# A graph-attention layer with residual norm on one core: two row buffers, copies put between signs, and positive sums that start on the first mask

## The chip, the cores and the metric

The kernel runs on one core of a Trainium2 chip. The metric is device time in microseconds (us), the median of several executions. The profile and the trace are those of one execution.

## The reference

One graph-attention layer over N = 8192 nodes with 256 features, H = 4 heads of 64 features, then a residual and a layer norm:

```python
xt  = einsum('ni,hio->hno', x, W)                    # 4 heads, 64 features each
src = einsum('hnf,hf->hn', xt, a[:, :64])
dst = einsum('hnf,hf->hn', xt, a[:, 64:])
e   = leaky_relu(src[:, :, None] + dst[:, None, :], 0.2)
e   = where(adj > 0, e, -inf)                        # adj is 8192 x 8192, int32
out = layernorm(x + concat_heads(softmax(e, axis=2) @ xt))
```

`exp(leaky_relu(s + d))` is a product of a factor of the row and a factor of the column, with one pair of factors where `s + d` is positive and another where it is not. So the kernel needs no exponential per edge: it splits the edges of a head by the sign of `s + d`, and sums the rows of two prepared tables (values and, as a 65th column, the denominators) over the positive and over the other edges.

## The kernel before

**Preparation.** About the first 216 us transform x, make the factors and write four tables of parts (V, 16 bit, a high and a low part of each number, for positive and for negative) to DRAM. The first adjacency blocks are converted, transposed and packed in AT.

**Main part.** The output rows are cut into NC = 8 chunks of 1024 rows. A chunk is done in H = 4 passes, one per head h, 32 passes in all. A pass has NG = 16 steps g, and a step handles 512 columns of the adjacency (B = 4 blocks of 128) for the chunk's 1024 rows. In each step:

- ScalarE (ACT, L392, `signs`) makes the sign of `s + d` for 4 blocks in an even step and for 3 in an odd one, in a ring `sgn` of NB = 4 steps. It may start step n when TensorE has ended the sums of step n-4 (`sums_done`).
- VectorE (DVE) makes the fourth block of an odd step (L552, `compares`), then the mask of the positive edges (L560, `masks_of`, `pos_done`), and last the mask of the others (L567, `rest_of`, `neg_done`). Between the two masks stand, in an even step, the comparison for the next step and one conversion of the next chunk's adjacency (L480, L482, `convert`), and in an odd step one `keep` (L496), which packs transposed blocks in AT.
- TensorE (PE), in an even step, first transposes the converted blocks (L719, `turn_masks`, waits for the conversion), and then multiplies: 64 matmuls of 128x128 masks by 128x130 of V (L754, `sums`): for each of 4 blocks and 8 row tiles t, one for the positive and one for the negative mask. They wait for `neg_done` of their step, which comes last.

**Between two passes.** The sums of pass p-1 lie in PSUM (`acc`) and have to be read before pass p may overwrite them. ScalarE copies the low parts to `u` in three portions (L405, `low`), after its step-1 signs of the new pass. Each portion waits for TensorE: the first two for `part_done` after 3/8 and 6/8 of the old step 15, the third for its end. VectorE adds the high parts (L574, `high`): portion 0 after its first mask of step 1, portions 1 and 2 after its second one. TensorE's step 0 waits for them one by one (`u_done`, before row tiles 0, 3 and 6). Then VectorE weighs, joins, inverts, divides and adds the residual (L582, L589, L593, L599, L608), one each in steps 2 to 6.

**Between two chunks.** One buffer `y` holds the chunk's x rows (loaded by a DMA of GpSimd's queue, L321, `load_res`), to which the four heads are added. In pass h = 0 of the next chunk VectorE takes the moments (L613, steps 8 and 9, and L619, step 10), GpSimd makes the scale and the shift (L327 to L333, `deviation`), ScalarE normalises 8 tiles, two after each of the steps 12 to 15 (L411, `normalise`, waits for `shift_done`), and GpSimd stores y (L337), waits for the store's landing and loads the next rows into the same buffer.

SyncE's queue loads V tables (one for each step), sign rows and adjacency blocks. The order on each engine is written out by hand. In the first chunk 10 or 11 blocks are converted and kept per pass in place of 8, and in the last one none.

Of the kernel before, what the change touches and what calls it, by code (L numbers as in the profile page):

```python
# [5 lines left out]
def gat_residual_norm(nc: bass.Bass, x: bass.AP, adj: bass.AP, W: bass.AP, a: bass.AP, out: bass.AP):  # L6
    fp32 = mybir.dt.float32
# [8 lines left out]
    ACT = mybir.ActivationFunctionType  # L16
# [30 lines left out]
    with ctx:  # L47
        def sb(name, shape, dt):
            return ctx.enter_context(nc.sbuf_tensor(name, shape, dt))

        def sem(name):
            return ctx.enter_context(nc.semaphore(name))
# [14 lines left out]
        shift = sb("shift", [P, T], fp32)  # L67
        big = sb("big", [P, 24144], fp32)

        def words(start, n):  # L70
            return big[:, start:start + n]
# [3 lines left out]
        sgn = words(8320, 4096).bitcast(i8).rearrange("p (n b i) -> p n b i", n=NB, b=B)  # L75
        y = words(12416, 2048).rearrange("p (t f) -> p t f", t=T)
        u = words(14464, 1040).rearrange("p (q v) -> p q v", v=VO)
# [67 lines left out]
        added = sem("added")  # L145
        res_in = sem("res_in")
        stats_done = sem("stats_done")
# [64 lines left out]
        def scalar_blocks(g):  # L212
            return B - g % 2
# [87 lines left out]
        def _(pool):  # L301
# [17 lines left out]

            def load_res(c):  # L320
                pool.dma_start(y[:, :, :], res_v[c]).then_inc(res_in, 16)  # L321

# [11 lines left out]

            def store(c):
                pool.wait_ge(norm_done, T * c + T)
                pool.dma_start(out_v[c], y[:, :, :]).then_inc(out_done, 16)  # L337
# [11 lines left out]
            with pool.Fori(1, NC) as c:  # L349
                chunk(c)  # L350
            deviation(NC - 1)
            store(NC - 1)
            pool.wait_ge(out_done, 16 * NC)


        @block.scalar
        def _(act):
# [29 lines left out]

            def signs(n, g, h):
                act.wait_ge(sums_done, n + 1)
                for b in range(scalar_blocks(g)):  # L390
                    r = (g * B + b) * H + h
                    ins = nc.scalar.activation(sgn[:, g % NB, b, :], srow[:, h % 2, :], ACT.Sign,  # L392
                                               bias=dflat[:, r:r + 1], scale=-1.0)
                ins.then_inc(sgn_done, 1)

# [11 lines left out]

            def normalise(c, ts):
                act.wait_ge(shift_done, 2 * c + 2)
                for t in ts:  # L410
                    nc.scalar.activation(y[:, t, :], y[:, t, :], ACT.Identity, bias=shift[:, t:t + 1],  # L411
                                         scale=rstd[:, t:t + 1]).then_inc(norm_done, 1)

            def chunk(c, first=False):
# [12 lines left out]
            act.wait_ge(lo_done, NG + 2)  # L427
            act.wait_ge(U2_done, 2 * NG)
            chunk(0, first=True)
            with act.Fori(1, NC) as c:  # L430
                chunk(c)
            for part in range(3):
                low(NP - 1, part)
            normalise(NC - 1, range(T))


        @block.vector
        def _(dve):
# [162 lines left out]

            def add_on(p, ec, eh):

                dve.wait_ge(res_in, 16 * ec + 16)
                dve.wait_ge(tr_done, p + 1)
                u4 = u.rearrange("p (t c) v -> p t c v", c=2)
                yh = y[:, :, eh * O:(eh + 1) * O]
                nc.vector.tensor_tensor(out=yh, in0=yh, in1=u4[:, :, 1, 0:O], op=ALU.add).then_inc(added, 1)  # L608

            def moments(c, ts):  # L610
                dve.wait_ge(added, 4 * c + 5)
                for t in ts:
                    nc.vector.bn_stats(stats[:, t, :], y[:, t, :]).then_inc(stats_done, 1)  # L613

# [7 lines left out]
            def chunk(c, plane, first=False, after_first=False, more=True):  # L622

                last = [UN * c + 2 * g + 4 for g in range(NG)]
                for h in range(H):
                    dve.wait_ge(row_in[h % 2], 32 * c + 16 * (h // 2 + 1))
                    for g in range(NG):
# [24 lines left out]
                        if ended:  # L652
                            if g == 1:
                                high(p, 1)
                                high(p, 2)
                            if g == 2:
                                weigh(p, ec, eh)
                            if g == 3:
                                join(p)
                            if g == 4:  # L660
                                inverse(p)
                            if g == 5:
                                divide(p)
                            if g == 6:
                                add_on(p, ec, eh)
                        if h == 0 and not first:
                            if g == 8:
                                moments(c - 1, range(0, 4))
                            if g == 9:
                                moments(c - 1, range(4, T))  # L670
                            if g == 10:
                                spread(c - 1)
# [13 lines left out]
            divide(NP - 1)  # L686
            add_on(NP - 1, NC - 1, H - 1)
            moments(NC - 1, range(T))
            spread(NC - 1)


        @block.tensor
        def _(pe):
# [118 lines left out]
```

## Time and profile before

| | |
|---|---|
| median of 3 runs | 2369.2 us (2365.97 to 2369.42) |
| profiled execution | 2367.08 us, span 2364.6 us |
| PE, DVE, ACT busy | 2108.9, 2098.4, 2012.6 us |
| matmuls L754, signs L392 | 32768, 1792 |
| TensorE's granted clock, mean | 0.962 |
| DMA, mean | 199 GB/s |

Rows of the windows view give busy times of each engine in a stretch. Rows of the timeline give start, duration, engine, line, operation, operands and count, and in brackets how long the engine had idled and who released it. A VectorE or ScalarE operation's duration overlaps the next one's start by about 0.1 us, so the distance of two starts is the better price.

### The profile page before, as it was taken

Reading aid. Unit: us, or ns where it says so; the run is one execution under the profiler, and the core shown is the slowest. Engines: PE = TensorE matmul, PEld = TensorE weight load, DVE = VectorE, ACT = ScalarE, POOL = GpSimd, SP = SyncE. Lnnn points to the kernel's source line nnn. Section 1 sums busy time; section 2 is a strip of 40 time slices with the busy share of each in tenths; the row PEclk is TensorE's granted clock in tenths of the full one; section 3 lists DMA queues with packets and bytes.
Section 4 is the critical chain, followed back from the end, with each engine's and each line's share of the span. In section 5 each row is a group of like instructions: output and inputs, shape, how many; then the busy total and the mean of one; then the engine's idle time right before and its main releaser. Section 6 shows DMA issues by size and latency. Waiting matters only on the chain.

```text
span 2364.6 us, 79642 instructions
## 1 busy us (share of the span) xinstructions
PE 2108.9 (89%) x34180; PEld 2063.9 (87%) x34180; DVE 2098.4 (89%) x2334; ACT 2012.6 (85%) x2045; POOL 120.0 (5%) x88
## 2 busy tenths in 40 slices
PE   7602999998999899998999999998999899998996
PEld 6502999998999899998999999998999899998996
DVE  4597999998999899998999899998999899987785
ACT  2235798898999899998999899998999899999995
POOL 0062000001000100001000100001000100001000
PEclk9855999999999999999999999999999999999998
DMA  8647776766666576666666576666666576533210
GB/s 296 221 180 284 275 247 231 241 218 213 209 200 221 176 239 208 209 202 212 211 199 209 188 236 205 213 203 209 210 203 221 176 236 206 194 84 105 84 52 19
DMA packets 236588, 469.77 MB, mean 199 GB/s; under 512 B 14656, under 2 KB 23104, under 8 KB 236224
## 3 DMA queue, kind: packets, MB, share of 16 engines
q1 hardware_dynamic: 231600, 447.53, 57.3%
q0 software_dynamic: 4352, 16.78, 2.0%
q8 instruction: 286, 4.69, 0.8%
q14 instruction: 78, 0.64, 0.1%
q10 hardware_dynamic: 272, 0.13, 0.0%
HBM read 438.83 MB, written 25.56 MB: 196 GB/s over the span
## 4 chain that ended last, share of the span: by engine, by line
PE 48%; ACT 16%; DVE 14%; issue 8%; POOL 2%; DVEq 0%; POOLq 0%; ACTq 0%
PE acc L754 46%; ACT big L392 15%; DVE big L560 4%; DVE big L567 4%; PE tp L719 2%; DVE nat L482 1%; ACT big L411 1%; DVE stats L613 1%; POOL shift L330 1%; DVE big L552 1%; DVE big L582 1%; DVE nat L480 1%; POOL rstd L329 0%; DVE AT L496 0%; DVE big L589 0%
## 5 line engine op out<-in xcount | busy, mean ns | idle before, releaser
L754 PE MATMUL acc<-big 128*128 128x130 f16 x32768 | 1933.5, 221 | 84.1 <-DVE big L567 53.7
L754 PEld LDWEIGHTS acc<-big 128*128 128x128 fp8e5 x32768 | 1901.0, 98 | 107.2 <-issue 103.6
L392 ACT ACTIVATE big<-big,d_all 128x1024 int8<-128x1024 f32 x1792 | 1881.4, 1139 | 60.9 <-PE acc L754 58.4
L560 DVE SCALAR_TENSOR_TENSOR big<-big,AT 128x1024 uint32<-128x1024 uint32 x512 | 627.4, 1225 | 168.6 <-ACT big L392 157.7
L567 DVE SCALAR_TENSOR_TENSOR big<-AT,big 128x1024 uint32<-128x1024 uint32 x512 | 627.0, 1225 | 4.5
L719 PE MATMUL tp<-ident,nat 128*128 128x128 f32 x1024 | 158.8, 278 | 133.0 <-DVE nat L480 115.9
L719 PEld LDWEIGHTS tp<-ident,nat 128*128 128x128 f32 x1024 | 109.7, 142 | 142.9 <-issue 132.5
L552 DVE TENSOR_SCALAR big<-big,d_all 128x1024 uint8<-128x1024 f32 x256 | 193.2, 755 | 0.0
L480 DVE TENSOR_SCALAR nat<-raw 128x2048 fp8e4<-128x2048 int32 x128 | 177.0, 1386 | 6.9 <-DMA raw<-in_adj_dram 6.5
L482 DVE TENSOR_SCALAR nat<-raw 128x2048 uint8<-128x2048 int32 x128 | 177.8, 1389 | 0.0
L496 DVE SCALAR_TENSOR_TENSOR AT<-AT,tp 128x512 uint32<-128x512 uint32 x224 | 154.8, 691 | 1.5
L405 ACT ACTIVATE big<-acc 128x390 f32<-128x390 f32 (+2 forms) x128 | 44.1, 382 | 76.0 <-PE acc L754 76.0
L327 POOL TENSOR_SCALAR rstd<-mv 128x8 f32<-128x8 f32 x8 | 7.3, 911 | 1925.0 <-DVE mv L619 1925.0
L411 ACT ACTIVATE big<-big,shift,rstd 128x256 f32<-128x256 f32 x64 | 34.3, 587 | 67.6 <-POOL shift L333 67.6
L385 ACT ACTIVATE big<-AT 128x1040 f16<-128x1040 f32 x16 | 17.4, 1088 | 62.4 <-POOL AT L318 42.3
L710 PE MATMUL acc<-big,AT 128*128 128x264 f32 x256 | 62.9, 401 | 4.2 <-DVE d_all L469 4.2
L710 PEld LDWEIGHTS acc<-big,AT 128*128 128x128 f32 x256 | 48.8, 196 | 15.5 <-issue 5.1
L467 DVE COPY big<-acc 128x1024 f32<-128x1024 f32 x16 | 19.6, 1225 | 39.4 <-PE acc L710 39.4
L574 DVE TENSOR_TENSOR big<-big,acc 128x390 f32<-128x390 f32 (+2 forms) x128 | 48.7, 424 | 6.0 <-ACT big L405 6.0
L363 ACT ACT_TABLE_LOAD x8 | 10.3, 1283 | 42.1 <-PE acc L702 42.1
L316 POOL TENSOR_TENSOR AT<-big 128x1024 f32 x16 | 38.7, 2421 | 40.2 <-DVE big L530 28.9
L582 DVE TENSOR_TENSOR big<-big,ab 128x1040 f32<-128x1040 f32 x32 | 39.7, 1241 | 0.0
(48 smaller groups left out, 364.2 us busy)
## 6 DMA issues: line engine op xcount, KB each, us to landing
raw<-in_adj_dram SPq DMA_DIRECT2D x256, 1024.0 KB, 5.4
big<-v_parts SPq DMA_DIRECT2D x512, 260.0 KB, 3.8
v_parts<-big SPq DMA_DIRECT2D x16, 1040.0 KB, 4.2
big<-s_rows SPq DMA_DIRECT2D x32, 512.0 KB, 5.8
AT<-in_x_dram SPq DMA_DIRECT2D x16, 512.0 KB, 4.0
big<-in_x_dram POOLq DMA_DIRECT2D x8, 1024.0 KB, 7.6
out_dram<-big POOLq DMA_DIRECT2D x8, 1024.0 KB, 7.9
big<-in_L_gnn_W_dram SPq DMA_DIRECT2D x2, 128.0 KB, 2.6
```

Of the source, the lines that this page charges most:

```text
L392: ins = nc.scalar.activation(sgn[:, g % NB, b, :], srow[:, h % 2, :], ACT.Sign, bias=dflat[:, r:r + 1], scale=-1.0)
L411: nc.scalar.activation(y[:, t, :], y[:, t, :], ACT.Identity, bias=shift[:, t:t + 1], scale=rstd[:, t:t + 1]).then_inc(norm_done, 1)
L480: nc.vector.tensor_scalar(to.bitcast(fp8e4), of, 0.0, 1.0, ALU.is_gt, ALU.add, saturate=False).then_inc(conv_done, 1)
L482: nc.vector.tensor_scalar(to, of, 0.0, 59.0, ALU.is_gt, ALU.add).then_inc(conv_done, 1)
L496: nc.vector.scalar_tensor_tensor(out=to, in0=to, scalar=EDGE[1 - plane], in1=of, op0=ALU.bitwise_and, op1=ALU.bitwise_or).then_inc(at_done, 1)
L552: ins = nc.vector.tensor_scalar(sgnu[:, g % NB, b, :], srow[:, h % 2, :], dflat[:, r:r + 1], 255.0, ALU.is_gt, ALU.mult)
L560: nc.vector.scalar_tensor_tensor(out=word(sgn, g % NB), in0=word(sgn, g % NB), scalar=EDGE[plane], in1=edges(g), op0=ALU.bitwise_and, op1= ...
L567: nc.vector.scalar_tensor_tensor(out=word(neg, g % NB), in0=edges(g), scalar=EDGE[plane], in1=word(sgn, g % NB), op0=ALU.bitwise_and, op1= ...
L582: nc.vector.tensor_tensor(out=u4, in0=u4, in1=w.unsqueeze(3).broadcast_to([P, T, 2, VO]), op=ALU.mult).then_inc(wu_done, 1)
L710: ins = nc.tensor.matmul(acc[:, 2 + b, 0:WX], xT[n][:, k, b, :], Wx[:, k, :], start=(k == 0), stop=(k == KF - 1))
L719: ins = nc.tensor.transpose(tp[:, u % 2, b * P:(b + 1) * P], natw[u % 2][:, b * P:(b + 1) * P], ident[:, :])
L754: return nc.tensor.matmul(acc[:, k, o:o + 2 * VO], m[:, g % NB, b, t * P:(t + 1) * P], Vr[:, v:v + 2 * VO], start=opens, stop=False, skip_ ...
```

## The change

Four edits:

1. **Two row buffers.** `y` becomes a pair, the second one in 2048 more words of `big`. `load_res(0)` and `load_res(1)` are both issued at the start, and after the store of chunk c the rows of chunk c+2 are loaded. `res_in` becomes two semaphores.
2. **Normalising later.** ScalarE normalises chunk c-1 in pass h = 1 of chunk c, one tile after each of the steps 8 to 15, where it was two tiles after each of the steps 12 to 15 of pass h = 0.
3. **Low copies between signs.** The three portions of `low` stand after the first, second and third sign of step 2, where they stood together ahead of step 2.
4. **Positive sums first.** In steps 1 to 14 TensorE does the 32 matmuls of the positive mask first and waits for `pos_done` alone, then waits for `neg_done` and does the 32 negative ones. Steps 0 and 15 keep their order and wait for both.

ScalarE's loop body has two chunks now (3 turns where there were 7), and so has GpSimd's.

```diff
-        y = words(12416, 2048).rearrange("p (t f) -> p t f", t=T)
+        y = [words(start, 2048).rearrange("p (t f) -> p t f", t=T) for start in (12416, 24144)]
...
             pool.wait_ge(U2_done, 2 * NG)
-            load_res(0)
+            load_res(0, 0)
+            load_res(1, 1)
 
-            def chunk(c):
-                deviation(c - 1)
-                store(c - 1)
-                pool.wait_ge(out_done, 16 * c)
-                load_res(c)
+            def chunk(c, n):
+                deviation(c)
+                store(c, n)
+
+                pool.wait_ge(out_done, 16 * c + 16)
+                load_res(c + 2, n)
...
-                        signs(p * NG + g, g, h)
-                        if g == 1 and not (first and h == 0):
-                            for part in range(3):
-                                low(p - 1, part)
-                        if g in (12, 13, 14, 15) and h == 0 and not first:
-                            normalise(c - 1, (2 * g - 24, 2 * g - 23))
+                        act.wait_ge(sums_done, p * NG + g + 1)
+                        for b in range(scalar_blocks(g)):
+                            ins = sign(g, h, b)
+                            if b == scalar_blocks(g) - 1:
+                                ins.then_inc(sgn_done, 1)
+                            if g == 2 and b < 3 and not (first and h == 0):
+                                low(p - 1, b)
+                        if h == 1 and g >= 8 and not first:
+                            normalise(c - 1, 1 - n, (g - 8,))
...
             def sums(p, g):
-                pe.wait_ge(neg_done, p * NG + g + 5)
+                pe.wait_ge(pos_done, p * NG + g + 1)
                 pe.wait_ge(v_in[g], 16 * p + 16)
...
                 else:
-                    for b in range(B):
-                        for cd in range(2):
+                    for cd in range(2):
+                        if cd:
+                            pe.wait_ge(neg_done, p * NG + g + 5)
+                            pe.sem_inc(pe_passed, 1)
+                        for b in range(B):
                             for t in range(T):
                                 ins = add(b, cd, t)
```

ScalarE at the start of a pass in the first chunk, before (L392 signs, L405 low copies; the second row of each pair is the rest of a step's signs):

```order
L392 ACTIVATE big<-big,d_all 128x1024 [waits sums_done,row_in0]
L392 ACTIVATE big<-big,d_all 128x1024 x3
L392 ACTIVATE big<-big,d_all 128x1024 [waits sums_done]
L392 ACTIVATE big<-big,d_all 128x1024 x2
L405 ACTIVATE big<-acc 128x390 [waits added,part_done]
L405 ACTIVATE big<-acc 128x390 [waits part_done]
L405 ACTIVATE big<-acc 128x195 [waits sums_done]
L405 ACTIVATE big<-acc 128x65
L392 ACTIVATE big<-big,d_all 128x1024 [waits sums_done]
L392 ACTIVATE big<-big,d_all 128x1024 x3
```

The same place in the changed kernel:

```order
L394 ACTIVATE big<-big,d_all 128x1024 [waits sums_done,row_in0]
L394 ACTIVATE big<-big,d_all 128x1024 x3
L394 ACTIVATE big<-big,d_all 128x1024 [waits sums_done]
L394 ACTIVATE big<-big,d_all 128x1024 x2
L394 ACTIVATE big<-big,d_all 128x1024 [waits sums_done]
L406 ACTIVATE big<-acc 128x390 [waits added,part_done]
L394 ACTIVATE big<-big,d_all 128x1024
L406 ACTIVATE big<-acc 128x390 [waits part_done]
L394 ACTIVATE big<-big,d_all 128x1024
L406 ACTIVATE big<-acc 128x195 [waits sums_done]
L406 ACTIVATE big<-acc 128x65
L394 ACTIVATE big<-big,d_all 128x1024
```

Three of the four signs of step 2 now stand ahead of the last low copy, and the fourth behind it.

TensorE in steps 0 to 2 of the second pass, before (L719 transposes, L754 sums):

```order
L754 MATMUL acc<-big 128x130 [waits neg_done,v_in0,u_done]
L754 MATMUL acc<-big 128x130 x23
L754 MATMUL acc<-big 128x130 [waits u_done]
L754 MATMUL acc<-big 128x130 x23
L754 MATMUL acc<-big 128x130 [waits u_done]
L754 MATMUL acc<-big 128x130 x15
L754 MATMUL acc<-big 128x130 [waits neg_done,v_in1]
L754 MATMUL acc<-big 128x130 x63
L719 MATMUL tp<-ident,nat 128x128 [waits at_done,conv_done]
L719 MATMUL tp<-ident,nat 128x128 x3
L754 MATMUL acc<-big 128x130 [waits neg_done,v_in2]
L754 MATMUL acc<-big 128x130 x63
```

The changed kernel in steps 0 to 2 of the second pass, from the last part of step 0 on:

```order
L760 MATMUL acc<-big 128x130 [waits u_done]
L760 MATMUL acc<-big 128x130 x15
L725 MATMUL tp<-ident,nat 128x128 [waits at_done,conv_done]
L725 MATMUL tp<-ident,nat 128x128 x3
L760 MATMUL acc<-big 128x130 [waits pos_done,v_in1]
L760 MATMUL acc<-big 128x130 x31
L760 MATMUL acc<-big 128x130 [waits neg_done]
L760 MATMUL acc<-big 128x130 x31
L760 MATMUL acc<-big 128x130 [waits pos_done,v_in2]
L760 MATMUL acc<-big 128x130 x31
L760 MATMUL acc<-big 128x130 [waits neg_done]
L760 MATMUL acc<-big 128x130 x31
```

A step's 64 matmuls are now two runs of 32 with a wait each, and where a step has transposes, they still stand ahead of both with their wait for the conversion.

## Rows read from the trace of the kernel before

**Rows 1.** Windows: window, length, busy us of PE, PEld, DVE, ACT, POOL, clock, DMA.
```profile
297.70:365.00 67.30, 64.43 (x1070) 63.00 (x1067) 65.19 (x71) 61.16 (x63) 0.00 (x0) 1.00 0.74 241
...
499.50:2095.10 1595.60, 1519.63 (x25340) 1495.51 (x25340) 1485.54 (x1656) 1462.13 (x1486) 50.99 (x36) 0.99 0.63 206
...
902.40:966.50 64.10, 62.79 (x1059) 61.85 (x1057) 60.70 (x66) 60.05 (x62) 0.00 (x0) 1.00 0.64 209
...
1030.60:1105.90 75.30, 66.41 (x1059) 64.47 (x1058) 63.52 (x81) 65.53 (x72) 8.17 (x6) 0.95 0.57 189
1105.90:1168.60 62.70, 62.06 (x1056) 61.83 (x1057) 62.29 (x67) 58.11 (x58) 0.65 (x1) 1.00 0.70 233
2095.10:2342.20 247.10, 236.34 (x4098) 235.08 (x4096) 190.04 (x209) 234.76 (x241) 7.37 (x6) 0.99 0.25 70
```
**Rows 2.** Waits of chunks 1 to 6 (499.5 to 2095.1): us in total, times, longest.
```profile
DVE big L560 <- ACT big L392: 104.1, 41, 4.8
...
ACT big L411 <- POOL shift L333: 53.6, 6, 9.4
ACT big L405 <- PE acc L754: 53.4, 53, 1.7
...
PE acc L754 <- DVE big L567: 45.5, 68, 3.8
...
PE acc L754 <- DVE big L574: 19.0, 14, 2.1
```
**Rows 3.** Timeline, one undisturbed pair of steps.
```profile
1003.46 7.39 ACT L392 ACTIVATE big<-big,d_all 128x1024 int8<-128x1024 f32 x7 [0.33 <-PE acc L754]
...
1006.40 1.24 DVE L560 SCALAR_TENSOR_TENSOR big<-big,AT 128x1024 uint32<-128x1024 uint32 x1
...
1007.34 7.44 PE L754 MATMUL acc<-big 128*128 128x130 f16 x128
...
1013.46 1.23 DVE L560 SCALAR_TENSOR_TENSOR big<-big,AT 128x1024 uint32<-128x1024 uint32 x1
```
**Rows 4.** Timeline, from pass h = 3 to pass h = 0 of the next chunk.
```profile
1028.01 0.50 ACT L405 ACTIVATE big<-acc 128x390 f32<-128x390 f32 x1 [1.51 <-PE acc L754]
...
1030.59 7.54 PE L754 MATMUL acc<-big 128*128 128x130 f16 x128
1030.68 36.50 ACT L392 ACTIVATE big<-big,d_all 128x1024 int8<-128x1024 f32 x35
1031.24 0.96 DVE L574 TENSOR_TENSOR big<-big,acc 128x390 f32<-128x390 f32 x3
1034.97 1.23 DVE L560 SCALAR_TENSOR_TENSOR big<-big,AT 128x1024 uint32<-128x1024 uint32 x1 [2.77 <-ACT big L392]
```
**Rows 5.** Timeline, the rest of that pass h = 0 and the start of h = 1.
```profile
1072.11 0.65 PE L719 MATMUL tp<-ident,nat 128*128 128x128 f32 x4 [0.52 <-DVE nat L480]
...
1073.30 7.43 PE L754 MATMUL acc<-big 128*128 128x130 f16 x128 [0.54 <-DVE big L567]
...
1081.22 1.09 ACT L411 ACTIVATE big<-big,shift,rstd 128x256 f32<-128x256 f32 x2 [9.44 <-POOL shift L333]
...
1088.64 6.41 PE L754 MATMUL acc<-big 128*128 128x130 f16 x64 [3.82 <-DVE big L567]
...
1102.84 1.18 ACT L405 ACTIVATE big<-acc 128x390 f32<-128x390 f32 x4
...
1108.10 6.13 PE L754 MATMUL acc<-big 128*128 128x130 f16 x104 [0.64 <-DVE big L574]
```
**Rows 6.** Last chunk: a wait of the timeline, and its sum over 2095.1 to 2342.2.
```profile
2139.43 1.09 ACT L411 ACTIVATE big<-big,shift,rstd 128x256 f32<-128x256 f32 x2 [3.25 <-POOL shift L333]
...
ACT big L405 <- PE acc L754: 9.2, 6, 6.3
```
**Rows 7.** The page: a group of part 5 and a DMA issue of part 6.
```profile
L363 ACT ACT_TABLE_LOAD x8 | 10.3, 1283 | 42.1 <-PE acc L702 42.1
...
big<-in_x_dram POOLq DMA_DIRECT2D x8, 1024.0 KB, 7.6
```

More of the change, by code:

```diff
@@ L67, in gat_residual_norm @@
         shift = sb("shift", [P, T], fp32)
-        big = sb("big", [P, 24144], fp32)
+        big = sb("big", [P, 26192], fp32)
         def words(start, n):
@@ L145, in gat_residual_norm @@
         added = sem("added")
-        res_in = sem("res_in")
+        res_in = [sem("res_in0"), sem("res_in1")]
         stats_done = sem("stats_done")
@@ L318, in _, with load_res @@
                     nc.gpsimd.tensor_copy(U2[n][:, :, :, O], e_row(e2, g)).then_inc(U2_done, 1)
-            def load_res(c):
-                pool.dma_start(y[:, :, :], res_v[c]).then_inc(res_in, 16)
+            def load_res(c, n):
+                pool.dma_start(y[n], res_v[c]).then_inc(res_in[n], 16)
             def deviation(c):
@@ L333, in deviation, with store @@
                 nc.gpsimd.tensor_tensor(out=shift[:, :], in0=shift[:, :], in1=rstd[:, :], op=ALU.mult).then_inc(shift_done, 1)
-            def store(c):
+            def store(c, n):
                 pool.wait_ge(norm_done, T * c + T)
-                pool.dma_start(out_v[c], y[:, :, :]).then_inc(out_done, 16)
+                pool.dma_start(out_v[c], y[n]).then_inc(out_done, 16)
             pool.wait_ge(lo_done, NG + 2)
             pool.wait_ge(U2_done, 2 * NG)
-            load_res(0)
-            def chunk(c):
-                deviation(c - 1)
-                store(c - 1)
-                pool.wait_ge(out_done, 16 * c)
-                load_res(c)
[L349 to L352, printed above, removed]
+            load_res(0, 0)
[5 more added lines that the diff above has]
+                load_res(c + 2, n)
+            with pool.Fori(0, NC // 2 - 1) as i:
+                chunk(2 * i, 0)
+                chunk(2 * i + 1, 1)
+            for c in (NC - 2, NC - 1):
+                deviation(c)
+                store(c, c % 2)
             pool.wait_ge(out_done, 16 * NC)
@@ L386, in _, with sign @@
                     nc.scalar.activation(V_part(n, 2), rows_of(U2[n]), ACT.Copy, scale=1.0 / LOW).then_inc(hi_done, 1)
[L388 to L394, printed above, removed]
+            def sign(g, h, b):
+                r = (g * B + b) * H + h
+                return nc.scalar.activation(sgn[:, g % NB, b, :], srow[:, h % 2, :], ACT.Sign,
+                                            bias=dflat[:, r:r + 1], scale=-1.0)
             def low(p, part):
@@ L406, in low, with normalise, chunk @@
                 ins.then_inc(low_done, 1)
-            def normalise(c, ts):
+            def normalise(c, n, ts):
                 act.wait_ge(shift_done, 2 * c + 2)
                 for t in ts:
-                    nc.scalar.activation(y[:, t, :], y[:, t, :], ACT.Identity, bias=shift[:, t:t + 1],
+                    nc.scalar.activation(y[n][:, t, :], y[n][:, t, :], ACT.Identity, bias=shift[:, t:t + 1],
                                          scale=rstd[:, t:t + 1]).then_inc(norm_done, 1)
-            def chunk(c, first=False):
+            def chunk(c, n, first=False):
                 for h in range(H):
@@ L428, in _ @@
             act.wait_ge(U2_done, 2 * NG)
-            chunk(0, first=True)
-            with act.Fori(1, NC) as c:
-                chunk(c)
+            chunk(0, 0, first=True)
+            with act.Fori(0, NC // 2 - 1) as i:
+                chunk(2 * i + 1, 1)
+                chunk(2 * i + 2, 0)
+            chunk(NC - 1, 1)
             for part in range(3):
                 low(NP - 1, part)
-            normalise(NC - 1, range(T))
+            normalise(NC - 1, (NC - 1) % 2, range(T))
         @block.vector
@@ L600, in divide, with add_on, moments @@
                                         in1=rden[:, :].unsqueeze(2).broadcast_to([P, T, O]), op=ALU.mult).then_inc(tr_done, 1)
-            def add_on(p, ec, eh):
-                dve.wait_ge(res_in, 16 * ec + 16)
+            def add_on(p, ec, eh, n):
+                dve.wait_ge(res_in[n], 8 * (ec - n) + 16)
                 dve.wait_ge(tr_done, p + 1)
                 u4 = u.rearrange("p (t c) v -> p t c v", c=2)
-                yh = y[:, :, eh * O:(eh + 1) * O]
+                yh = y[n][:, :, eh * O:(eh + 1) * O]
                 nc.vector.tensor_tensor(out=yh, in0=yh, in1=u4[:, :, 1, 0:O], op=ALU.add).then_inc(added, 1)
-            def moments(c, ts):
+            def moments(c, n, ts):
                 dve.wait_ge(added, 4 * c + 5)
                 for t in ts:
-                    nc.vector.bn_stats(stats[:, t, :], y[:, t, :]).then_inc(stats_done, 1)
+                    nc.vector.bn_stats(stats[:, t, :], y[n][:, t, :]).then_inc(stats_done, 1)
             def spread(c):
@@ L664, in chunk @@
                             if g == 6:
-                                add_on(p, ec, eh)
+                                add_on(p, ec, eh, 1 - plane if h == 0 else plane)
                         if h == 0 and not first:
                             if g == 8:
-                                moments(c - 1, range(0, 4))
+                                moments(c - 1, 1 - plane, range(0, 4))
                             if g == 9:
-                                moments(c - 1, range(4, T))
+                                moments(c - 1, 1 - plane, range(4, T))
                             if g == 10:
@@ L686, in _ @@
             divide(NP - 1)
-            add_on(NP - 1, NC - 1, H - 1)
-            moments(NC - 1, range(T))
+            add_on(NP - 1, NC - 1, H - 1, 1)
+            moments(NC - 1, 1, range(T))
             spread(NC - 1)
```

2 lines of the change are left out of this document (added).

## Prediction
> **What bounds the kernel now.** I read the windows view first, cut where a pass of TensorE starts. The six chunks 1 to 6 take 1595.6 us, 265.9 each, and they are two thirds of the time [rows 1]. Inside a chunk the four passes differ, and that is the point to see: h = 0 takes 75.3 us, h = 1 takes 62.7, and h = 2 (and h = 3, with the same length) 64.1 [rows 1].
>
> Next I asked what each engine would need alone. **TensorE:** the h = 1 pass holds a single wait inside, 0.64 us [rows 5], so a pass without waits is 62.70 - 0.64 = 62.06 us, a chunk 248.2. **VectorE:** a pair of steps, from the first mask of an even step to the next one with no idle time, is 1013.46 - 1006.40 = 7.06 us [rows 3], 56.5 for 8 pairs. The six pieces of work on the old pass add some 4.5 (VectorE is busy 60.7 in h = 2 [rows 1]), the moments about 3.2 more in h = 0: about 247 per chunk. **ScalarE:** 35 signs run in 36.50 [rows 4], 1.043 each, so 56 are 58.4. Four low copies in a row take 1.18 and two normalised tiles 1.09 [rows 5], so a chunk is 4 x 59.6 + 8 x 0.54 = 242.7. So all three have nearly the same load, TensorE's being the largest, and the 17.7 us above it in each chunk (265.9 - 248.2) are waits that go round between the engines.
>
> The waits view says which [rows 2]: ScalarE waits 53.6 us for the shift, in 6 waits of some 9, and 53.4 for TensorE ahead of the low copies. VectorE waits 104.1 for signs. TensorE waits 45.5 and 19.0 for VectorE. The timeline shows the two places. At a pass boundary ScalarE is done with step 1, waits 1.51 for the first portion and more for the others, and starts the signs of step 2 only at 1030.68. VectorE, which has ended its high parts by then, idles 2.77 until 1034.97 [rows 4]. It then has 7.06 us of work per pair against TensorE's 7.76 (62.06/8) plus the work on the old pass, so it can't make it up, and TensorE loses 2.0 per pass (64.1 - 62.06). In h = 0 ScalarE stands 9.44 us in front of its first normalised tile, VectorE starves, TensorE idles 3.82, and its next 64 matmuls take 6.41 us where 128 usually take 7.44 [rows 3, 5].
>
> **The change part by part.** *Normalising in h = 1* (edit 2; edit 1 makes it possible, since the buffer is needed for the next chunk otherwise). The shift is ready two thirds through h = 0, so the wait of about 9 goes whole. The 4.4 us of normalising stay on ScalarE, one pass later. In h = 0 the excess over the bare pass is 75.3 - 62.06 = 13.2. One part remains: VectorE's moments make it late for step 10, where TensorE waits 0.52 + 0.54 [rows 5]. I keep 1.1.
>
> *Low copies between signs* (edit 3). ScalarE's three waits at the boundary are now filled by signs it would have had to do anyway. It may start step 2 when the old step 14 ends, a step (half of 7.44) and four transposes (0.5) before step 0 of the new pass, at 1026.4. Four signs and the copies then end by 1032.5 against 1034.9, so VectorE's wait of 2.77 shrinks to some 0.3. That is the shape the h = 1 pass has today (four copies without waits at 1102.84, and no stall behind the one of 0.64) [rows 5]. So in h = 2 and h = 3 the 2.0 us go.
>
> *What comes instead.* In h = 1 ScalarE gets 4.3 us more, and regains 0.46 per pair (7.76 - 7.30 for 7 signs), 1.8 over these four. It arrives at h = 2 late by 2.5. VectorE then is late with the high parts, which TensorE's step 0 waits for. It ends portion 1 at 1031.24 + 0.47 = 1031.7, and row tile 3 is due 24 matmuls after 1030.59, at 1032.0 [rows 4], a slack of 0.3; in steps 0 and 1 about 0.5 is regained. So TensorE loses 2.5 - 0.3 - 0.5 = 1.7 there. The moments also leave VectorE late at the boundary to h = 1. After step 10 three pairs regain 2.1 of some 3.2, and I take 0.8 for what is left over the slack. A chunk becomes 248.2 + 1.1 + 0.8 + 1.7 = 251.8, a gain of 14.1, times six 84.6.
>
> *Positive sums first* (edit 4). It lets a step start on the first mask, and the second one may come 32 matmuls later (1.9 us). In an even step, though, the sums stand behind transposes that wait for the conversion, which comes just ahead of the second mask, so there the gain is under 1 us of slack. In odd steps the conversion is not in the way. By the steps above most of the 45.5 us that TensorE waits for the second mask [rows 2] are gone already, so I count this edit nothing by itself (bounds 0 and -1 per pass). Of its cost: the same matmul count; a slot of PSUM is revisited after 8 matmuls where it was 16, while steps 0 and 1 together (step 0 revisits after 2) take 7.54 against 7.44 for an ordinary pair [rows 3, 4], so 0 to 0.1 per step. 8 is nearer to 16 in effect, since the inner loop is unchanged, and I take 0; the other end, 0.1 x 14 x 32 = 45 us, is a rival. The extra wait in the middle I price at 0: step 0 has two such waits and is at most that 0.1 longer.
>
> *Last chunk.* No conversions, so ScalarE sets the pace (busy 234.8 of 247.1 [rows 1]). Its waits go: 3.25 for the shift, 9.2 - 7.2 = 2.0 at the three inner boundaries (the rest of the 9.2 is the end of the program) [rows 6], and 2.8 at the first boundary, as in rows 4. Gain 8. *First chunk.* VectorE is the bound (65.2 of 67.3 [rows 1]), and only its idle time for signs at the boundaries goes: 3 in three passes. *Second load at the start:* 1 MB, 7.6 us to landing [rows 7], while adjacency and V loads are waited for; between 0 and 7.6, I take 1. The end of the program is as before.
>
> Sum against the profiled execution: 2367.1 - 84.6 - 8 - 3 + 1 = 2272.5. The median lies 2.1 above that execution, so I give **2274**.
>
> **The clock.** In h = 0, which holds the shift wait, the mean clock is 0.95, in h = 1 and h = 2 it is 1.00 [rows 1]. After 3.82 us idle 64 matmuls took 6.41 [rows 5], 100 ns each against 58 (7.44 for 128 [rows 3]), so most of them ran at the 1.2 GHz level; the waits for high parts, up to 2.1 [rows 2], lie at the start of h = 1 and leave it at 1.00. The waits that I leave are at most 1.7, so no drop is in the sum. The Trainium skill ("TensorE: Matmul & The Clock Gate", Part 1) says that idleness takes TensorE to half clock and that activity gives it back. By that rule the trace agrees, and should a remaining wait cost a drop per chunk, 2.7 us each by rows 5, the sum would be 16 higher.
>
> **The rivals.**
> - *Everything is hidden.* VectorE's slack may be larger than I read, since edit 4 loosens it. Then a chunk is 248.2: 106 for six, 9 and 5 elsewhere, **2250**. For it: the h = 1 pass of today. Against: the moments' stall at step 10 waits for a conversion, which edit 4 does not touch.
> - *ScalarE's backlog stays.* Its reserve is 5.5 us per chunk; if copies between signs cost more than in a row, the 2.5 us of h = 1 are not regained and each of three further boundaries costs 1.5. Chunk 256.3: 58 for six, **2306**.
> - *Slower matmuls* by the revisit after 8, as priced above, up to 45: **2319** at most, 2296 halfway.
> - *The shift wait is only moved* (the second buffer does not free ScalarE, since a store or load is late): the chunk keeps its 265.9 and only the low copies gain, which VectorE loses again: no change. Against it: the normalising now stands 20 steps behind the moments.
> - *Slower: function tables.* ScalarE alternates between Sign and Copy or Identity. Per chunk there are 4 x 6 + 16 = 40 such switches where there were 16. Would each load a table for 1.283 us [rows 7], ScalarE's chunk would be 242.7 + 51 = 294, 28 over today's chunk: **2560**. The point where it turns slower is 18 loads per chunk. Against it: the 8 loads of this trace all have line L363, in the preparation, although 16 switches per chunk are there already. The Trainium skill ("ScalarE activation tables: per-element evaluation and per-set limits", "What a function is on this engine") says that functions of different sets are one load of 1283 ns apart and that those of one set need no switch. By that rule the three functions share a set, the trace agrees, and it adds nothing.
>
> **How the numbers follow.** Forecast, 2260 to 2290: 0.62. Everything hidden: 0.14. Backlog: 0.15. Slower matmuls: 0.05. Only moved: 0.02. Function tables: 0.02. Change and no change can be told apart at 0.2%, 4.7 us; all cases but the last two lie below 2364, so faster 0.96, same 0.02, slower 0.02. The range reaches from the first rival (2250) to just short of the backlog's 2306: 2250 to 2302, with the forecast, the hidden case and a part of the backlog's in it.
>
> **What would show it.** Right: the h = 0 pass near 63.2, h = 1 near 62.9, h = 2 near 63.8, h = 3 near 62.1; no ScalarE wait for the shift except the last; its wait ahead of the low copies near nothing; VectorE's wait for signs under 30 us in chunks 1 to 6; clock 1.00 throughout; still 8 table loads. Wrong: passes of 64 or more in h = 2 and 3 (backlog), more than 7.5 us per 128 matmuls (revisit), or a wait of TensorE in the middle of steps.

## The result, and the profile after

The changed kernel takes 2387.3 us (median of 4 runs, 2381.95 to 2399.94) against 2368.7 for the kernel before: a ratio of 1.0088, 95% interval 1.0047 to 1.013. It is slower by about 0.9%, where 4% faster was forecast. The profiled execution is the longest of the four, 2399.9 us with a span of 2398.1. Its spread of 18 us is new as well; the kernel before had 3.5.

The windows view of the changed kernel, cut at the starts of TensorE's passes as in [rows 1] (columns as there): first the second pass of chunk 0, then chunks 1 to 6 together, one pass each of h = 2, h = 0 and h = 1, and the last chunk.

```profile
298.40:363.60 65.20, 63.50 (x1071) 63.03 (x1069) 65.20 (x71) 61.51 (x64) 0.00 (x0) 1.00 0.75 249
495.90:2134.20 1638.30, 1530.12 (x25343) 1519.41 (x25342) 1492.70 (x1656) 1466.62 (x1489) 58.63 (x36) 0.97 0.62 201
907.70:976.30 68.60, 63.73 (x1058) 63.27 (x1058) 63.56 (x68) 61.67 (x62) 0.00 (x0) 0.97 0.65 205
1044.60:1112.60 68.00, 63.58 (x1058) 63.12 (x1059) 63.86 (x81) 60.30 (x60) 8.10 (x4) 0.98 0.62 197
1112.60:1180.90 68.30, 63.71 (x1058) 63.26 (x1058) 60.15 (x65) 62.30 (x67) 1.86 (x2) 0.97 0.67 213
2134.20:2376.20 242.00, 235.30 (x4096) 234.53 (x4094) 190.37 (x209) 231.51 (x239) 6.48 (x5) 0.99 0.24 67
```

The pattern of before (75.3, 62.7, 64.1) is gone. Every pass of chunks 1 to 6 now takes about 68 us, whatever its h. The first and the last chunk are shorter than before. So the loss has nothing to do with heads, moments or normalising: it is the same 5 to 6 us in each of the 24 passes of the middle, on top of the 62 to 63 a pass should take.

The waits of chunks 1 to 6, to be laid beside [rows 2]:

```profile
ACT big L394 <- PE acc L760: 167.1, 159, 7.7
DVE big L566 <- ACT big L394: 142.6, 103, 6.2
PEld tp L725 <- issue: 107.0, 23, 5.9
PE tp L725 <- issue: 91.6, 21, 4.7
```

ScalarE's waits for the shift (53.6) and ahead of the low copies (53.4) have vanished, and so have TensorE's for VectorE (45.5 and 19.0). In their place TensorE idles 91.6 us in 21 waits that end with an "issue": nothing in the profile was missing, its own queue had not yet handed out the next instruction. ScalarE and VectorE then wait for TensorE. The timeline of the boundary that ends pass h = 3:

```profile
1034.81 4.35 PE L760 MATMUL acc<-big 128*128 128x130 f16 x72
...
1036.87 0.50 ACT L406 ACTIVATE big<-acc 128x390 f32<-128x390 f32 x1 [0.25 <-PE acc L760]
...
1041.22 1.23 DVE L566 SCALAR_TENSOR_TENSOR big<-big,AT 128x1024 uint32<-128x1024 uint32 x1 [0.55 <-ACT big L394]
...
1043.73 0.74 PE L725 MATMUL tp<-ident,nat 128*128 128x128 f32 x4 [4.57 <-issue]
...
1044.54 8.91 PE L760 MATMUL acc<-big 128*128 128x130 f16 x128
...
1049.86 7.39 ACT L394 ACTIVATE big<-big,d_all 128x1024 int8<-128x1024 f32 x7 [5.56 <-PE acc L760]
```

The steps of the prediction are all there: the low copies no longer wait (0.25 for 1.51), and VectorE's idle time before step 2 is 0.55 for 2.77 [rows 4]. But TensorE stands still for 4.57 us between the last sum of the old pass and the first transpose of the new one. Its next 128 matmuls take 8.91 us for 7.54, and the granted clock of these passes is 0.97 to 0.98, where it was 1.00 in h = 1 and h = 2 before.

At that point of the code there is only one thing: the back edge of TensorE's loop over the passes (L794, L783 in the kernel before). The query for one line shows its instructions on TensorE's queue (count, then duration in ns as min/median/max). The kernel before:

```profile
L783 PEldq COMPARE_BRANCH  x24: 88/358/1329, 569.3 to 2094.1; - x24
```

The changed kernel:

```profile
L794 PEldq COMPARE_BRANCH  x24: 88/5140/6483, 557.2 to 2132.8; - x24
```

The branch takes 5.14 us where it took 0.36. The 24th is the exit. And TensorE's queue for instructions has moved more, though the same matmuls are issued; the page of the kernel before and of the changed one:

```profile
q8 instruction: 286, 4.69, 0.8%
```

```profile
q8 instruction: 309, 5.06, 0.8%
```

That is 23 packets of 16 KB more, as many as the main loop has taken back edges. Of the four edits only edit 4 touches TensorE's program. It gives each of the 16 steps a second wait with its semaphore instruction (steps 0 and 15 have both ahead of their sums), and the body needs 4 register operations more: it grows from 2169 to 2189 records of TensorE and its queue. The transposes are not moved. The order rows ahead of the prediction could suggest it, since they show transposes ahead of step 2 for the kernel before and ahead of step 1 for the changed one; but in the second pass both kernels have them ahead of step 1 (at 302.17 and 302.86 us).

### The profile page after: what moved, and what is told of

It reads as the page before. It is cut to its first block, busy times and chain, and to the rows that moved or that the text cites. A ratio compares the mean times of both kernels' runs of the same rounds, so it can differ in the third digit from the quotient of the medians.

```text
span 2398.1 us, 80165 instructions
## 1 busy us (share of the span) xinstructions
PE 2115.4 (88%) x34180; PEld 2086.6 (87%) x34180; DVE 2105.3 (88%) x2334; ACT 2015.4 (84%) x2045; POOL 127.6 (5%) x88
## 4 chain that ended last, share of the span: by engine, by line
PE 58%; DVE 12%; ACT 10%; issue 9%; DVEq 0%; POOL 0%; ACTq 0%; POOLq 0%
PE acc L760 55%; ACT big L394 9%; DVE big L566 4%; PE tp L725 4%; DVE big L573 4%; DVE nat L488 1%; DVE big L558 1%; ACT big L412 1%; DVE AT L502 1%; DVE nat L486 1%; DVE stats L619 0%; DVE big L580 0%; ACT big L406 0%; DVE big L588 0%; DVE big L614 0%
## 5 line engine op out<-in xcount | busy, mean ns | idle before, releaser
L760 PEld LDWEIGHTS acc<-big 128*128 128x128 fp8e5 x32768 | 1923.8, 99 | 25.6 <-issue 22.5
L725 PE MATMUL tp<-ident,nat 128*128 128x128 f32 x1024 | 163.8, 285 | 228.0 <-DVE nat L486 116.4
## 6 DMA issues: line engine op xcount, KB each, us to landing
big<-in_L_gnn_W_dram SPq DMA_DIRECT2D x2, 128.0 KB, 2.6
```

Source lines behind the costliest of these rows:

```text
L725: ins = nc.tensor.transpose(tp[:, u % 2, b * P:(b + 1) * P], natw[u % 2][:, b * P:(b + 1) * P], ident[:, :])
L760: return nc.tensor.matmul(acc[:, k, o:o + 2 * VO], m[:, g % NB, b, t * P:(t + 1) * P], Vr[:, v:v + 2 * VO], start=opens, stop=False, skip_ ...
```

## Experiments

All times are medians beside runs of the kernel before on the same chip (2366 to 2368 us).

### Which edit, and whether it is the branch

**e1: edits 1 to 3 without edit 4.** The changed kernel with `sums` as it was before:

```diff
-                pe.wait_ge(pos_done, p * NG + g + 1)
+                pe.wait_ge(neg_done, p * NG + g + 5)
...
                 if g in (0, NG - 1):
-                    pe.wait_ge(neg_done, p * NG + g + 5)
-                    pe.sem_inc(pe_passed, 1)
...
-                    for cd in range(2):
-                        if cd:
-                            pe.wait_ge(neg_done, p * NG + g + 5)
-                            pe.sem_inc(pe_passed, 1)
-                        for b in range(B):
+                    for b in range(B):
+                        for cd in range(2):
```

> Edits 1 to 3 alone (two row buffers, late normalising, copies between signs); TensorE's sums in the order of before. Theory A: the lost time is at the back edge of TensorE's loop, where the branch takes 5.1 us in place of 0.36 since edit 4 made the loop body 20 instructions longer and moved it; then this kernel has no such stall, its branch takes 0.36 us, and it comes near 2274 us (2255 to 2300), the sum of the prediction. Rival B: the copies between signs or the late normalising make the stall at the pass boundary; then it stays at 2380 to 2400.

Measured: 2273.44 us, ratio 0.9603 (0.9587 to 0.9619). Its branch:

```profile
L789 PEldq COMPARE_BRANCH  x24: 88/363/1217, 559.3 to 2009.3; - x24
```

Its windows: chunks 1 to 6, one pass each of h = 2, h = 3, h = 0 and h = 1.

```profile
496.80:2009.80 1513.00, 1493.59 (x25341) 1483.83 (x25338) 1485.75 (x1657) 1462.05 (x1488) 57.90 (x36) 1.00 0.67 217
875.80:938.50 62.70, 62.00 (x1056) 61.56 (x1055) 62.48 (x68) 60.58 (x62) 0.90 (x1) 1.00 0.72 233
938.50:1000.40 61.90, 61.90 (x1059) 61.81 (x1058) 61.18 (x66) 60.01 (x61) 0.00 (x0) 1.00 0.67 212
1000.40:1063.90 63.50, 62.45 (x1060) 61.98 (x1059) 62.95 (x80) 60.17 (x61) 7.72 (x4) 1.00 0.66 210
1063.90:1127.40 63.50, 62.77 (x1060) 62.05 (x1058) 61.13 (x66) 62.84 (x68) 1.19 (x2) 1.00 0.68 226
```

Theory A holds, B falls. Edits 1 to 3 give what the sum said: 1513.0 for the six chunks where it had 1595.6 - 84.6 = 1511.0. Against these, the changed kernel's 1638.3 is 125.3 us more, 5.2 for each of 24 passes. (Both are profiled executions, and each is the longest of its four; by the medians the two kernels are 113.8 us apart.) VectorE's waits for signs in these chunks fall to 24.0 us, where under 30 was forecast.

**e4: edit 4 alone, on the kernel before.**

> The kernel before with edit 4 alone (positive sums first, one wait more per step). Theory A: the branch takes some 5 us in each of the 24 passes of the loop, 2400 to 2480 us. Rival B (edits 1 to 3 make the stall): 2355 to 2375.

Measured: 2442.18 us, ratio 1.0317 (1.0274 to 1.036), branch median 4.93 us. So edit 4 carries the loss alone, and on the kernel before, which gains nothing from the other edits, it shows in full.

### What about edit 4 makes the branch slow

Length of the body, its place in the instruction stream, or the wait in the middle of a step? Idle semaphore increments ahead of the loops move the body without changing it. TensorE issues them in the preparation, where it idles 110.7 us, so they cost nothing:

```diff
             pe.wait_ge(sT_done, 1)
+            for _ in range(192):
+                pe.sem_inc(pe_passed, 1)
```

**e2: the changed kernel with 192 of them.**

> The changed kernel with 192 semaphore increments that do nothing, put on TensorE ahead of its loops, where it has some 100 us of idle time. The body of the loop is as long as in the changed kernel, but it begins at another place of the instruction stream. The instruction queue fetches 16 KB pieces, 256 instructions; counted in the trace, the loop head of before stands at 219 of 256 and that of the changed kernel at 27; this one puts it at 219. Theory A1 (place decides): branch 0.4 us, about 2275 us. Theory A2 (length of the body decides, 2189 against 2169): the stall stays, 2385 to 2400.

Measured: 2283.2 us, ratio 0.9646 (0.9626 to 0.9665). The rows of its two loops, the main one and that of the last chunk:

```profile
L796 PEldq COMPARE_BRANCH  x24: 88/418/1437, 559.4 to 2009.1; - x24
...
L798 PEldq COMPARE_BRANCH  x4: 88/3160/3577, 2068.8 to 2258.1; - x4
```

The same code, with edit 4 and its longer body, is over 100 us faster by being moved. So length (A2) and the wait in the middle are out. The small loop, though, stalls in its three turns here, with a median of 3.16 us.

**e3: the kernel before with 64 of them.**

> The kernel before with 64 such increments ahead of the loops: the body is unchanged at 2169 instructions, its head moves from 219 to 27 of 256, the place of the changed kernel. Theory A1 (place decides): the branch takes about 5 us in every pass, and the time goes up by some 24 x 3 to 24 x 6 us less what the present waits at the boundary hide, 2400 to 2480. Theory A2 (length decides): 2368, no change.

Measured: 2373.1 us, ratio 1.0027 (1.0015 to 1.0038).

```profile
L785 PEldq COMPARE_BRANCH  x24: 88/358/477, 567.3 to 2091.9; - x24
...
L787 PEldq COMPARE_BRANCH  x4: 88/2359/4357, 2158.9 to 2344.0; - x4
```

A miss: with the loop's head at the place of the changed kernel nothing happened in the main loop, and only the small loop began to stall. So it is the place, but not that of the head. I laid the ends of the bodies side by side, where the branch stands, counted from the trace in program order, modulo 256. A packet holds 16 KB, and where the main part is straight code (e9 below) there are 69815 records of TensorE and its queue to 270 packets, 259 to a packet, which fits 256 instructions of 64 bytes. The zero of the count is arbitrary, since it starts at the first recorded instruction; I put the kernel before at 84. What is put ahead of the loops moves a branch by its number, and the first branch of the small loop comes 2090 records behind the last one of the main loop (2110 with edit 4).

| branch at | kernel, loop | median us |
|---|---|---|
| 84, 84, 104 | before, e1, e2, main loops | 0.36, 0.36, 0.42 |
| 126, 148 | before's small loop, e3 main | 0.35, 0.36 |
| 166 | e2 small | 3.16 |
| 168, 168 | changed main, e4 main | 5.14, 4.93 |
| 190 | e3 small | 2.36 |
| 230, 230 | changed small, e4 small | 1.45, 2.27 |

The expectations of e5 and e6 have other places for the small loops (155 for 126, 188 for 166, 208 for 190, 3 or 4 for 230); the main loops are right to 1, and the rule is the same by either count.

That is a rule that the first four runs had not been made for: a branch that stands early in its piece is slow, and a piece seems to begin somewhere between 148 and 166 of my count. By this count the changed kernel's branch has just crossed into a new piece; the border itself is in no record. (The medians of the small loops are over 4 branches, one of which is the exit.)

**e5: the kernel before with 84 increments,** which puts its branch at the changed kernel's place.

> The kernel before with 84 idle semaphore increments ahead of TensorE's loops. Theory A3, from the runs so far: what decides is where in its 256-instruction piece the branch at the END of the body stands. By my count of the trace (zero arbitrary) branches at 84, 85, 105, 147, 148 and 155 took 0.36 us, and branches at 167, 168, 188, 208 and 3 took 2 to 6 us. This kernel has its branch at 168, the place of the changed kernel, with the body and the order of before: so 5 us in each pass, 2420 to 2460 us, as with edit 4 alone (2442). If the longer body or the wait in the middle of the step is needed for the stall: 2367 to 2375.

Measured: 2437.25 us, ratio 1.0295 (1.0274 to 1.0316).

```profile
L785 PEldq COMPARE_BRANCH  x24: 87/4876/6891, 567.9 to 2163.8; - x24
```

This is the cleanest of the runs. The kernel before, with not one instruction of its main part changed, loses 70 us by 84 idle instructions ahead of it, where 64 cost it 5. It also takes edit 4 out of the explanation: 2437 here, 2442 with edit 4 alone.

**e6: the changed kernel with 128 increments.**

> The changed kernel with 128 idle increments ahead of the loops: the branch of the main loop comes to 40, that of the last chunk's loop to 132 of 256, both outside the stretch from 160 to 3 (or a little further) that stalls. Theory A3: 24 branches and the 3 of the last chunk near 0.4 us; 2268 to 2278 us. If edit 4 costs something of its own (or the 10 us by which e2 lies above e1 are not the last chunk's branches of 3.3 us): 2280 or more. If edit 4 gains something of its own: below 2268.

Measured: 2275.17 us, ratio 0.961 (0.9594 to 0.9626).

```profile
L796 PEldq COMPARE_BRANCH  x24: 88/378/2142, 559.1 to 2009.8; - x24
...
L798 PEldq COMPARE_BRANCH  x4: 88/352/362, 2068.5 to 2251.2; - x4
```

The medians of both loops are near 0.36 again, and the whole change, edit 4 included, is 3.9% faster. The main branch stands at 40 and the small loop's at 102 (not 132). Not every turn is free: every fourth main branch of e6, six in all, takes 1.8 to 2.1 us. At 84 (e1) the same turns take 0.8 to 1.2.

**e11: the changed kernel with 60 increments,** for the size of the stall further on in the piece.

> The changed kernel with 60 idle increments ahead of the loops: the branch moves from 168 to 228 of 256, some 65 instructions behind the point (about 161) where the stall begins. If the fetch of the target starts only when the piece that holds the branch is entered, the stall shortens by the time of 60 instructions, 30 pairs of 57 ns, 1.7 us: branch 3.4 us, and the kernel comes to about 2335 (2310 to 2350). If the stall were all or nothing: 5.1 us and 2387.

Measured: 2353.49 us, ratio 0.995 (0.9933 to 0.9966).

```profile
L796 PEldq COMPARE_BRANCH  x24: 88/2253/3243, 558.2 to 2076.6; - x24
```

Shorter, not all or nothing: 5.14 falls to 2.25, more than the 1.7 expected. The time is a miss all the same, 2353 with a range of 2310 to 2350; the runs of this kernel spread over 23 us, and the profiled one is the shortest (2341.67).

What sets the length can be read from the start of each 16 KB packet in the traces. The twelve kernels with loops have 312 taken branches. Each of the 165 that took over 0.7 us ended 2.3 to 3.3 us, mostly 2.4, after such a packet had started. For the 147 shorter ones the last packet had started at least 1.8 us before the branch. In the changed kernel that packet starts 2.7 us after the branch does, in e11 0.1 us before it (medians), and this is the difference of the two stalls. So a slow branch goes with a late packet. Why the packet comes 2.8 us earlier in e11, where 60 instructions are worth 1.7, is open.

**e10: e1 without the branch prefetch hint** (`hint_back_edge=False` on both loops).

> Edits 1 to 3 (as e1) with the branch prefetch hint of TensorE's two loops taken away; the body is one instruction shorter. If the hint is what makes the branch cheap at the places where it is cheap, every branch now takes about 5 us, as in the changed kernel: 2360 to 2400. If the queue finds the target by itself: 2273.

Measured: 2406.64 us, ratio 1.0162 (1.0142 to 1.0182).

```profile
L789 PEldq COMPARE_BRANCH  x24: 79/5391/6967, 558.8 to 2136.6; - x24
```

Without the hint the branch costs 5.39 us even at the good place, with 311 packets in place of 286 on the queue of instructions. So the hint is what makes the branch cheap in e1, and in the changed kernel, at 5.14 us, it gained next to nothing. The time lies 7 us above the range expected. The Trainium skill ("Runtime: NRT & Kernel Launch", section "Instruction fetch mechanics") says that instructions come in 16 KiB blocks of 256, fetched in sequence, and that a taken branch to a block not at hand forces a fetch. By that rule e10 is the plain case. The packets of 16 KB in the trace agree with the size.

**e9: the changed kernel with the passes of TensorE written out.**

```diff
-            with nc.Fori(H, NP - H, engines=PE, hint_back_edge=True) as p:
+            for p in range(H, NP - H):
                 one_pass(p, lambda g: [((p + H) * HALF + g // 2, g // 2)] if g % 2 == 0 else [])
-            with nc.Fori(NP - H, NP, engines=PE, hint_back_edge=True) as p:
+            for p in range(NP - H, NP):
                 one_pass(p, lambda g: [])
```

> The changed kernel with TensorE's 28 looped passes written out, so that TensorE has no back edge in the main part, and every wait is against a constant. The instructions executed are the same but for the loop's own. If the loop's branch is the whole difference between the sum of the prediction and the measured time: 2268 to 2278 us, and no idle time of TensorE that ends with an issue at the pass boundaries. If straight code of some 60000 instructions is fetched too slowly: above 2290.

Measured: 2271.57 us (2270.1 to 2273.5), ratio 0.9591 (0.9575 to 0.9607). The queue of instructions moves 270 packets, fewer than in any kernel with the loops (286 to 311), and the granted clock is 0.968 for 0.948. Only one wait of a matmul in it ends with an issue, of 1.0 us. So straight code is fetched without a stall of note, and this version does not depend on where a branch falls. Of the kernels run, it has the lowest median.

### What each edit is worth

**e12: e9 without edit 4.**

> Edits 1 to 3 with TensorE's passes written out, so no back edge: the twin of e9 (2271.57 us) without edit 4. It prices edit 4 by itself. Prediction's term: nothing, so 2268 to 2276. If positive sums first is worth something when no branch is in the way: above 2278. If its waits cost something: below 2266.

Measured: 2273.31 us (2271.98 to 2274.16), ratio 0.9607 (0.9594 to 0.962). With the branch out of the way edit 4 is worth 1.7 us by the medians, and the intervals of the two ratios overlap: nothing that these runs can tell apart.

**e7: edits 1 and 2 alone** (low copies back in their place, and `sums` of before as in e1, not shown again):

```diff
-                            if g == 2 and b < 3 and not (first and h == 0):
-                                low(p - 1, b)
+                        if g == 1 and not (first and h == 0):
+                            for part in range(3):
+                                low(p - 1, part)
...
```

> Edits 1 and 2 alone: two row buffers and normalising in pass h = 1; low copies where they were, sums as before. By the terms of the prediction the shift wait (9 us) and what follows from it go, the 2.0 us per boundary of the copies stay, and h = 2 gets the late start of 1.7: a chunk of about 258.8 against 265.9, 43 us for six, 2325 (2310 to 2340). If the clock drop was a larger part of the old loss, lower.

Measured: 2317.06 us, ratio 0.9786 (0.9769 to 0.9802), 51 us gained for 43. Its passes h = 2, 3, 0 and 1:

```profile
889.50:952.30 62.80, 62.05 (x1055) 61.72 (x1056) 61.99 (x67) 58.75 (x59) 0.90 (x1) 1.00 0.72 233
952.30:1016.40 64.10, 62.79 (x1059) 61.84 (x1057) 61.18 (x66) 60.05 (x61) 0.00 (x0) 1.00 0.64 207
1016.40:1082.40 66.00, 63.32 (x1059) 61.83 (x1056) 63.22 (x81) 60.04 (x61) 7.72 (x4) 1.00 0.62 200
1082.40:1147.60 65.20, 63.14 (x1058) 61.81 (x1056) 61.14 (x66) 64.61 (x71) 0.97 (x1) 1.00 0.67 221
```

h = 0 falls from 75.3 to 66.0, and a chunk comes to 258.1, where I had 258.8. Surprising is h = 2: 62.8, for 65.8 by the terms (62.06 + 2.0 + 1.7). But h = 1 takes 65.2, for 62.9, and the two together 128.0, for 128.6. A part of this is where the windows are cut: TensorE waits 1.00 us for the high parts just ahead of the cut at 889.5, and that falls to h = 1. ScalarE comes to this boundary late after the normalising and waits only 0.44 us, ahead of its third low copy, so the two costs overlap.

**e8: edit 3 alone** (`low` between the signs of step 2, on the kernel before).

> Edit 3 alone: low copies between the signs of step 2, everything else as before. By the terms of the prediction h = 2 and h = 3 lose their 2.0 us each, h = 0 gains at most 1, since ScalarE only comes earlier to the wait for the shift: 5 per chunk, 2338 (2325 to 2350).

Measured: 2324.9 us, ratio 0.9819 (0.9803 to 0.9835), 43 us gained for 30, just outside the range. The wait for the shift is still there in full (65.7 us of ScalarE over the program, 67.6 before). The two gains, 51 and 43, add up to the 94 of e1, so together they give what each gives alone. The 43 and 30 expected of them add up to 73, too little for the 94 that the sum had right: the split of the gain was less well forecast than the whole.


## Why the prediction was wrong, step by step

- **What bounds the kernel: right.** Three engines with about 62 us per pass, TensorE's 62.06 as the floor, and waits of 17.7 per chunk. e1 reaches 252.2 per chunk (1513.0/6), and its h = 3 pass takes 61.9.
- **Normalising in h = 1, low copies between signs: right together, in size and in place.** Passes forecast at 63.2, 62.9, 63.8 and 62.1 (h = 0 to 3) took 63.5, 63.5, 62.7 and 61.9 in e1. A chunk was to take 251.8 and takes 252.2. Of the two wrong ones, the late start of h = 2 (1.7) is only some 0.7, and h = 1 loses 0.6 more than it was given.
- **First and last chunk: right.** The second pass of chunk 0 takes 65.2 in place of 67.3 (2.1 us gained, where I had 1). The last chunk takes 242.0 in place of 247.1 with a stalling loop and 239.7 without (e9, from the chunk's first matmul to its last), where I had 239.
- **The sum for edits 1 to 3: right.** 2274 forecast, 2273.4 measured (e1), and 2271.6 with edit 4 and no loop (e9).
- **Positive sums first: the step that failed.** "The extra wait in the middle I price at 0" is true of the wait as such: in chunks 1 to 6 of the changed kernel no sum of TensorE waits for VectorE, and e12 against e9 shows no cost. But I weighed only what the instruction does when it is issued. What it does by standing there, 20 instructions more in a loop body and 64 more ahead of it, I did not ask. It moved the loop's branch to another place in the instruction stream, by my count just over the border of a 16 KB piece, and that made each of 23 back edges 4.8 us longer (5.14 - 0.36). With the slow clock behind it and less the waits it covers, it is 5.2 us in each of 24 passes, the whole 125.3 us between the profiled middle parts of e1 and the changed kernel. That it is the place and nothing else of edit 4 is shown by e5 (the place without the edit: 70 us lost) and e6 (the edit at another place: nothing lost). The branch could be read in the trace of before, at 0.36 us with 1.33 once, and I didn't ask what keeps it short.
- **The clock: right as a mechanism, wrong in the sum.** "The waits that I leave are at most 1.7, so no drop is in the sum." The new wait is 4.6, and behind it 128 matmuls take 8.91 in place of 7.54: 1.4 us of the 5.2.
- **The rivals.** Everything hidden and the backlog are both out by e1. The shift wait that is only moved is out: no wait of ScalarE for the shift is left in chunks 1 to 6. The function tables are out: 8 loads, all in the preparation. Slower matmuls by the revisit of PSUM after 8 are out: two steps in the new order take 7.42 in the timeline of the changed kernel, with 7.44 before [rows 3]. The rival that ended slower was the wrong one; none of them looked at the code that TensorE fetches. The row of the changed kernel's timeline:

```profile
1061.43 7.42 PE L760 MATMUL acc<-big 128*128 128x130 f16 x128
```

What stays open: why the packet that a slow branch goes with starts late where the branch stands early in its piece, hint or no hint, and why 60 instructions further on it starts earlier by more than their own time. Bodies of lengths other than 2169 and 2189 were not tried in the main loop.

## What to carry to other kernels

An edit to a long hardware loop has a second effect besides what its instructions do: it moves the loop's branch in the instruction stream, and here that alone was worth up to 4.8 us per turn (0.36 against 5.14). After any edit of such a body, read the loop's own line in the profile (the branch's duration, and the idle time of the first instruction behind it that ends with an "issue") before judging the edit, and compare at a place where the branch is cheap, or with the loop written out. When every turn loses the same time, whatever work it does, look at what the turns have in common.

## What the runs showed of the hardware

- A taken back edge of TensorE's loop of some 2170 instructions took 0.36 us with the prefetch hint and 5.39 without it (e1 and e10, medians).
- With the hint its median was 0.35 to 0.42 us wherever the branch was counted from 40 to 148 of 256 instructions, and 1.45 to 5.14 from 166 to 230, the longest at 168 (table above, e5, e6, e11). At 34 (small loop of e11) two turns took 0.45 and one 3.47.
- A branch over 0.7 us ended 2.3 to 3.3 us after the start of a 16 KB packet of instructions, in 165 of 165 cases (all kernels with loops).
- A wait of this kind can stand behind a loop as well: in e1's profiled execution, the slowest of its four, TensorE idled 3.39 us with an "issue" in step 0 of the last chunk, from 3 us behind the exit of the main loop on, and went on 2.7 us after a packet had started. Whether the loop's end is its cause is not shown. The timeline row is

```profile
2015.74 61.31 PE L760 MATMUL acc<-big 128*128 128x130 f16 x1024 [3.39 <-issue]
```

- Straight code of 28 passes, over 60000 instructions, was fetched with no "issue" wait of a matmul over 1.0 us (e9), with 270 packets of instructions against 309 for the same code with the loops, or 286 in e1.
